# A depthwise 5x5 convolution on TensorE: 24 tiles of up to 128 pixels a plane for 25 squares of 121, and the stores issued by ACT

## What is computed

```python
def reference(x, L0_conv_kernel):           # x (128, 55, 55, 96), kernel (96, 5, 5)
    k = jnp.transpose(kernel, (1, 2, 0))[:, :, None, :]
    y = lax.conv_general_dilated(x, k, window_strides=(1, 1), padding='SAME',
        dimension_numbers=('NHWC', 'HWIO', 'NHWC'), feature_group_count=96)
    return x + y
```

## Time and profile before

| | us |
|---|---|
| median of 3 runs | 821.78 (820.1 to 821.82) |
| the profiled execution | 820.36 |
| its span, first to last instruction | 818.6 |
| PE busy in it | 811.2 (99%), 7217 products |
| POOL, ACT, DVE busy | 620.6, 617.4, 538.9 |
| mean granted TensorE clock | 0.999 |

### The profile page before, as it was taken

How to read it: one execution, slowest core, us unless ns; L and a number is a source line. 1 busy time by engine, 2 the same in 40 slices (tenths; PEclk the granted TensorE clock), 3 DMA queues, 4 the chain that set the end, 5 groups by cost and what they waited for, 6 DMA issues and landing times.

```text
span 818.6 us, 19694 instructions
## 1 busy us (share of the span) xinstructions
PE 811.2 (99%) x7217; PEld 809.2 (99%) x7217; DVE 538.9 (66%) x2224; ACT 617.4 (75%) x1157; POOL 620.6 (76%) x263
## 2 busy tenths in 40 slices
PE   8999999999999999999999999999999999999997
PEld 7999999999999999999999999999999999999997
DVE  6666666666666666666666666666666666666664
ACT  6777777777777777777777777777777777777774
POOL 2978878778696786977778878778696786977772
PEclk9999999999999999999999999999999999999999
DMA  9999999999999999999999999999999999999965
GB/s 370 418 414 393 388 387 386 392 385 396 395 389 393 375 402 388 387 391 383 395 391 391 389 386 386 395 381 395 395 387 394 380 399 381 390 390 391 389 246 232
DMA packets 32497, 313.40 MB, mean 383 GB/s; under 512 B 3600, under 2 KB 6800, under 8 KB 8080
## 3 DMA queue, kind: packets, MB, share of 16 engines
q1 hardware_dynamic: 31968, 311.67, 97.4%
q10 hardware_dynamic: 432, 0.46, 0.2%
HBM read 161.13 MB, written 150.99 MB: 381 GB/s over the span
## 4 chain that ended last, share of the span: by engine, by line
PE 98%; DMA 1%; DVE 0%; ACT 0%; ACTq 0%; issue 0%; DVEq 0%
PE sums L428 98%; DMA places_in<-places 1%; DVE x_low L254 0%; DVE weights L249 0%; DVE rest L235 0%; DVE taps_split L233 0%; DVE taps_split L237 0%; ACT y_out L323 0%; ACTq L219 0%; DVEq L163 0%; DVE y_out L357 0%; DVEq L228 0%
## 5 line engine op out<-in xcount | busy, mean ns | idle before, releaser
L428 PE MATMUL sums<-weights,x_high 121*128 121x226 f32 (+3 forms) x4800 | 804.1, 274 | 0.0
L428 PEld LDWEIGHTS sums<-weights,x_high 121*128 121x128 f32 x4800 | 729.0, 192 | 0.0
L428 PE MATMUL sums<-weights,x_low 121*128 121x226 f32 (+3 forms) x2400 | 659.1, 275 | 1.5 <-DVE x_low L254 1.5
L254 POOL TENSOR_TENSOR x_low<-x_in,x_high 121x1920 fp32r<-121x1920 f32 x95 | 411.9, 4336 | 175.3 <-ACT x_high L315 175.3
L323 ACT ACTIVATE y_out<-sums 128x264 f32<-128x264 f32 (+2 forms) x960 | 360.4, 398 | 189.8 <-PE sums L428 176.0
L428 PEld LDWEIGHTS sums<-weights,x_low 121*128 121x128 f32 x2400 | 460.8, 192 | 1.9 <-issue 1.9
L363 DVE TENSOR_TENSOR y_out<-sums,y_out 128x96 f32<-128x96 f32 (+3 forms) x1056 | 263.0, 249 | 123.3 <-ACT y_out L323 102.3
L315 ACT ACTIVATE x_high<-x_in 121x1920 fp32r<-121x1920 f32 (+1 forms) x195 | 295.2, 1514 | 5.3 <-DMA x_in<-x 5.2
L254 DVE TENSOR_TENSOR x_low<-x_in,x_high 121x1280 fp32r<-121x1280 f32 (+1 forms) x100 | 170.1, 1704 | 71.1 <-ACT x_high L315 71.1
L357 DVE TENSOR_TENSOR y_out<-sums,y_out 128x44 f32<-128x44 f32 (+2 forms) x768 | 152.0, 198 | 76.6 <-ACT y_out L323 76.3
L249 POOL TENSOR_TENSOR weights<-taps_split,places_in 121x450 fp32r<-121x450 f32 x95 | 133.7, 1407 | 7.2 <-DVE taps_split L237 7.2
(11 more groups left out here) (9 smaller groups left out, 1.9 us busy)
## 6 DMA issues: line engine op xcount, KB each, us to landing
x_in<-x SPq DMA_DIRECT2D x95, 1600.0 KB, 11.6
y<-y_out SPq DMA_DIRECT2D x95, 1536.0 KB, 7.5
taps_in<-taps SPq DMA_DIRECT2D x22, 150.0 KB, 11.8
x_in<-x SPq DMA_DIRECT2D x5, 320.0 KB, 5.3
y<-y_out SPq DMA_DIRECT2D x3, 302.5 KB, 2.5
y<-y_out SPq DMA_DIRECT2D x1, 357.5 KB, 3.7
taps_in<-taps ACTq DMA_DIRECT2D x2, 150.0 KB, 4.9
y<-y_out SPq DMA_DIRECT2D x1, 271.0 KB, 2.6
```

Source lines behind the costliest of these rows:

```text
L254: engine.tensor_tensor(x_low[slot][0:SQUARE, cols], x_in[c % X_SLOTS][0:SQUARE, cols], x_high[slot][0:SQUARE, cols].bitcast(F32), ALU.subt ...
L428: product = pe.matmul(sums, v[slot][0:SQUARE, at:at + IMAGES], window, start=n == 0 and v is x_low, stop=n == len(squares) - 1 and part == ...
```

## The change

A plane is cut into three bands of 16 rows by seven strips of 8 columns, 128 pixels each (the last strip has 7 columns), and a foot, rows 48 to 54, in three tiles of 7 x 18 = 126 pixels. One pixel column is left at the foot's right end, 7 pixels of column 54: the corner. The corner doesn't go through PE: for a group of channels at once DVE (for the first four channels POOL) multiplies its pixels with the taps and adds up, in twelve steps (a memset, five times a product and an addition, the pixels themselves), and the result is added to y_out as the last operation of every channel. 24 tiles make 72 products a channel, in 12 sums, ten copied by ACT and two by DVE. y_out is now in the plane's own order.

Windows of the blocks are 20 x 12, those of the foot 9 x 25 (written by POOL in two more operations, 25 columns in a pitch of 26). The taps' split moves from POOL to DVE, one of its three operations in each of three channels out of four. DVE's corner steps stand behind the sixth, ninth and twelfth sum of a channel: three a channel in the first four channels, one or two up to channel 11, then one in each channel up to 83, none from 84 on. The stores of all channels but the last move from SP to ACT, behind the first copy of the next channel. At the start one load brings the first taps, the centre and the block mask; the foot's mask and the corner's pixels and taps (1.08 MB) follow on ACT's queue; POOL does the twelve corner steps of the first group before its first windows and makes the last two x_low pieces of channel 0. 14 products of zeros for 17.

```diff
-SIDE = 11
-GRID = HEIGHT // SIDE
+BLOCK_H, BLOCK_W = 16, 8
+BANDS = 3
+STRIPS = 7
+FOOT = BLOCK_H * BANDS
+FOOT_H, FOOT_W = HEIGHT - FOOT, 18
+FOOT_TILES = 3
...
+GROUPS = ((0, 4), (4, 12)) + tuple((c, c + 12) for c in range(12, CHANNELS, 12))
+CORNER_STEPS = 2 + 2 * TAPS
...
+SUMS = ((0, (0, 1, 2)), (0, (3, 4)), (0, (5, 6)),
+        (1, (0, 1)), (1, (2, 3)), (1, (4, 5)), (1, (6,)),
+        (2, (0, 1)), (2, (2, 3)), (2, (4, 5)), (2, (6,)),
+        (BANDS, (0, 1, 2)))
...
-FIRST_PIECES = tuple((j, j + 1) for j in range(GRID))
-LATER_PIECES = ((0, 2), (2, GRID))
+FIRST_PIECES = ((0, 3), (3, 7), (7, 14), (14, 21), (21, 24))
+LATER_PIECES = ((0, 11), (11, 24))
...
+        def place_foot(engine, c):
...
+            for part in (HIGH, LOW):
...
+                engine.tensor_tensor(window, turned, mask, ALU.mult).then_inc(foot_ready[c % SLOTS], 1)
...
+        def sum_corner(engine, group, step):
...
+            if adds:
+                to = sums[:, :, row:end_row, :]
+                engine.tensor_tensor(to, part, to, ALU.add).then_inc(corner_step[group > 0], 1)
+            else:
...
+                engine.tensor_tensor(part, pixels[:, :, row + shift:end_row + shift].unsqueeze(3).broadcast_to(shape),
+                                     rows.unsqueeze(2).broadcast_to(shape), ALU.mult).then_inc(corner_step[group > 0], 1)
...
         @block.sync
...
-                store_y(c)
...
         @block.scalar
...
+            def store_y(c):
+
+                act.wait_ge(tile_copied, copied(c, LAST_SUM))
+                act.wait_ge(y_step, stepped(c, LAST_SUM))
+                act.dma_start(out[c, :, :], y_out[c % Y_SLOTS][:, :]).then_inc(y_stored[c % Y_SLOTS], 16)
...
                             copy_sums(c, i)
+                            if i == 0 and c > 0:
+
+                                store_y(c - 1)
...
         @block.vector
...
+                    part = corner_sum[group % GROUP_SLOTS][:, c - GROUPS[group][0], :, :]
+                    seam = y[:, HEIGHT - CORNER_ROWS:HEIGHT, WIDTH - CORNER_OUT:WIDTH]
+                    dve.tensor_tensor(seam, part, seam, ALU.add).then_inc(y_step, 1)
...
+                if c // BATCH + 1 < BATCHES and c % BATCH < SPLIT_STEPS:
+                    split_taps(dve, c // BATCH + 1, c % BATCH)
+                for i in range(len(SUMS)):
                     finish_sums(c, i)
+                    if i in (5, 8, 11) and todo:
+                        sum_corner(dve, group + 1, todo.pop(0))
```

More of the change, by code:

```diff
@@ new lines, with rows_of, cols_of, pitch_of @@
+Y_COLS = 3072
+def rows_of(i):
+    band = SUMS[i][0]
+    return max(0, band * BLOCK_H - HALO), min(HEIGHT, (band + 1) * BLOCK_H + HALO)
+def cols_of(i):
+    band, strips = SUMS[i]
+    width = FOOT_W if band == BANDS else BLOCK_W
+    return max(0, width * strips[0] - HALO), min(WIDTH, width * (strips[-1] + 1) + HALO)
+def pitch_of(i):
+    first, end = cols_of(i)
+    return end - first + (end - first) % 2
+def tiles_of(i):
+    band, strips = SUMS[i]
+    return [band * STRIPS + strip for strip in strips]
@@ L93, with copied_by_act, row_seam, col_seam @@
+def copied_by_act(i):
+    return i not in (6, 10)
+def row_seam(i):
+    return SUMS[i][0] > 0
+def col_seam(i):
+    return SUMS[i][1][0] > 0
+LAST_SUM = len(SUMS) - 1
+COPIES = [sum(copied_by_act(n) for n in range(i + 1)) for i in range(len(SUMS))]
+STEPS = [sum((not copied_by_act(n)) + row_seam(n) + col_seam(n) + (n == LAST_SUM) for n in range(i + 1))
+         for i in range(len(SUMS))]
 COPIES_ALL, STEPS_ALL = COPIES[-1], STEPS[-1]
@@ L152, in bank_of, with group_of, build @@
 def bank_of(c, i):
-    return (c * len(TILES) + i) % BANKS
-LAST_TILE = len(TILES) - 1
+    return (c * len(SUMS) + i) % BANKS
+def group_of(c):
+    return next(g for g, (first, end) in enumerate(GROUPS) if first <= c < end)
 LAST = CHANNELS - 1
-LAST_STORES = tuple((Y_AT[j], Y_AT[j + 1] if j < GRID - 1 else Y_COLS) for j in range(GRID))
-def build(nc, x, taps, places, out):
+LAST_STORES = ((6, 0, WIDTH * (2 * BLOCK_H - HALO)),
+               (10, WIDTH * (2 * BLOCK_H - HALO), WIDTH * (FOOT - HALO)),
+               (11, WIDTH * (FOOT - HALO), Y_COLS))
+def build(nc, x, taps, start, foot, corner, out):
     with ExitStack() as ctx:
@@ L173, in build @@
         y_out = [sbuf(f"y_out{i}", [P, Y_COLS], F32) for i in range(Y_SLOTS)]
[L174 to L177, removed]
+        start_in = sbuf("start_in", [P, 2 * BATCH_COLS + BLOCK_COLS], F32)
@@ L428, in tile @@
-                        product = pe.matmul(sums, v[slot][0:SQUARE, at:at + IMAGES], window,
+                        if foot_tile:
+                            window = foot_weights[slot][0:pixels, part, :, left:right]
+                        else:
+                            window = block_weights[slot][:, part, :].rearrange("p (r c) -> p r c", c=WINDOW_W)[
+                                :, above:above + end - first, left:right]
+                        product = pe.matmul(sums, v[slot][0:pixels, at:at + IMAGES], window,
@@ L443, in _ @@
                     pe.wait_ge(low_ready[slot], lows(c, piece))
[L444 to L446 removed]
+                    for i in range(len(SUMS)):
+                        if first <= tiles_of(i)[0] < end:
+                            sum_tiles(c, i)
 def lay_out_input(x):
[L450 to L451 removed]
```

436 lines of the change are left out of this document (246 added, 190 removed).

## The result

The changed kernel takes **923.29 us** (median of 4 runs, 922.75 to 923.73), the kernel before in the same comparison 821.06. The ratio is 1.1246 with a 95% interval of 1.1226 to 1.1265: 12.5% slower. The prediction was 941, with a range of 838 to 965.

The account below looks back on a forecast made before the run. PE's loads of x bound the kernel before; in the changed one a circle over ACT, POOL and DVE was expected. 9.6 + 14 + 697 + 126 + 88 + 4.6 + 1.8 = 941 us, range 838 to 965.

Parts of the forecast that it names:

- channel 0: First channel: POOL waits for the corner data, so its x_low comes after PE wants it; 14 us.
- channels 1 to 84: 70 channels with a two-operand corner step at 9.95 us, 14 with or behind a memset step at 9.0.
- The circle: Corner step waits out POOL's x_low, delaying ACT's store, x_high and the next x_low; 9.95 us a channel, chance 0.68.
- Memset channels and those behind them: 7 channels whose corner step is a memset and the 7 behind them: between 8.04 and 9.95, taken at 9.0.
- A PE clock that stays at full in spite of such gaps: Sign for the forecast: PE's clock stays full although PE waits 1.9 us once a channel.
- 24 tiles, 8.04 a channel: PE: 72 products a channel at 111.7 ns each, 8.04 us for 8.38; over 96 channels 32 us less.
- Two signs: ACT idle some 2 us before the copy behind the store; PE waiting 1.9 us a channel for a DVE seam.
- The DMA, counted at nothing: 8.04 us a channel asks for 398 GB/s; the queues were expected to give it, so nothing was counted.
- The foot's windows, 0.60 each: POOL's two new window operations: 0.60 us each, between bounds of 0.52 and 1.43.
- third rival: Foot's windows cost 1.43 us each or more, POOL and DVE share 10.3 us a channel; about 970 us, chance 0.04.
- The second rival: DVE blocked but no circle; POOL and DVE's shared SBUF time paces, 8.67 a channel, 846 us; 0.14 including mixtures.
- The first rival: Corner steps get in beside POOL or cost DVE nothing it can't catch up; 794 us, chance 0.14.

Follow-up runs that it names:

- e2: The changed kernel with DVE's corner steps moved ahead of all seams, stores still by ACT: 820.44 us, ratio 0.999 to the kernel before.
- e3: The changed kernel with the steps of DVE's corner groups replaced by memsets in the same places, from channel 4 on: 797.45 us.
- e6: The kernel before, stores by ACT, plus one DVE instruction of 252 columns a channel, both operands in SBUF, result unused: 1021.56 us.
- e8: As e6, stores by ACT, but the added instruction's first operand is in PSUM: 820.50 us.
- e1: The changed kernel with its stores issued by SP again, nothing else: 853.99 us, ratio 1.040 to the kernel before.
- e7: As e6, both operands in SBUF, but the stores stay with SP as in the kernel before: 951.49 us.
- e5: The changed kernel with corner steps ahead of the seams, a first group of 12 channels and a new start, stores by ACT: 803.72 us.
- e4: The kernel before, changed only in that ACT issues the stores behind the next channel's first copy: 821.08 us.

## Why the prediction was right, point by point

The mechanism is the one that was put down, and e2, e3, e6 and e8 show it: take away the place, the kind of instruction or the second SBUF operand, and the loss goes. The terms of the sum against what was measured in the profiled execution:

| term | predicted, us | measured, us |
|---|---|---|
| first product | 9.6 | 8.5 |
| channel 0 | 14 | 16.4 |
| channels 1 to 84 | 823 | 803.9 |
| the last 11 | 88 | 89.2 |
| tail and around the span | 6.4 | 5.5 |
| sum (the profiled execution) | 941 | 923.4 |

- **The circle, 9.95: 9.68.** The mis-sized terms are ACT's. The issue took 0.34, not 0.45. For the four copies 1.48 stood, the length of the rows end to end; but an instruction's row on ACT begins before the one ahead has ended (the four copies' row runs to 509.91, the x_high behind them starts at 509.76), so from start to start they took 1.11. x_high was 1.62 for 1.59, POOL's x_low 3.76 as computed, the corner step's end 0.25 behind it for 0.28, DVE's tail 2.38 for 2.29. The 70 channels that were taken at 9.95, by 0.27 less, make 19 us; the sum was too high by 18, so the other terms cancel nearly. The circle's lower bound, 914, held; of its two bounds, 9.6 and 10.2 for 70 channels are 916 and 958, not 914 and 962.
- **Memset channels and those behind them** were taken at 9.0 each: 8.46 and 9.03.
- **Channel 0, 14: 16.4.** POOL's start was as described, and PE waited 4.4 us once for POOL's x_low. What was not foreseen is that the clock fell there.
- **"A PE clock that stays at full in spite of such gaps"** failed at the start. The granted clock fell to half (1.2 GHz) three times in the first 130 us of the span, for 3.4 to 6.8 us; in three stretches of 4 us that end near the falls (12 to 16, 54 to 58, 122 to 126) PE had been busy for only 2.5, 2.5 and 2.4. That alone doesn't tell a fall: from 502.24 to 506.24 it was 2.50 too, and the clock stayed at full. What decides is not shown. Behind the third fall it stayed at full up to the last product, though PE was busy for 87% of the stretch from 100 to 700 us only; mean 0.992. In e6, with a longer wait each turn (PE stood 1.69 us at 512.78 there, 1.50 at 506.24 here), it fell, in parts of the run, every 20 us for 3.4, mean 0.957. There a channel of 11.95 us is followed by one of 8.7 or 8.8, together two turns of 10.33: PE's slower stretch was covered by the circle, which runs over ACT, POOL and DVE.
- **24 tiles, 8.04 a channel:** 8.05 to 8.08 where nothing holds PE up. 111.7 ns held for 240 columns too (median 112 from product to product in e3).
- **Two signs came at another size.** ACT stood idle for 2.8 and 3.4 us ahead of the copy behind the store (the turns at 499.01 and 508.65), not for some 2, and PE waited for a seam of DVE for 1.3 in the mean (98.0 us in 75 waits), not for 1.9.
- **The DMA, counted at nothing:** right, e3 moved 398 GB/s.
- **The foot's windows, 0.60 each:** 0.79 in the mean, 0.65 alone, so the third rival was far off. POOL has the room.
- **The second rival, 846 at 8.67 a channel,** came close to e1 (853.99 at 8.7), but not for its reason. It counted what DVE and POOL share as the bound; in e1 POOL still stood idle for 187 us waiting for x_high, and e7 shows that what remains without ACT's store is a circle over PE's banks, with a length of its own. That it is this circle is read from the chains of e1 and e7; no run takes it apart. The prediction had not named it, and the expectation for e7 failed on that.
- **The first rival, 794,** is what the change would have given without the exclusion: 797.45 in e3.

What stays open: the 16.4 us of channel 0 in the changed kernel were not taken apart into POOL's lateness and the clock's, and whether the last 6 us of e5 can be had by another order of DVE's three instructions wasn't tried.

## What to carry to other kernels

Before an instruction is put behind another on DVE, look for its operands: with both in SBUF it should not come up while a long instruction of POOL runs (4.00 us for 0.42 in e6); with one operand in PSUM (e8), or as a memset (e3), it was not held off at the same place. Such a stall is dear only where it closes a circle, so follow the late engine's result until it comes back: here once over the store on ACT, once over PE's banks, and the longer one sets the time. A sum of busy times, or even of the times that DVE and POOL exclude each other, finds neither; and the remedy was not to remove work or to move the store back, but to move the step some places forward in its own engine's order.

## What the runs showed of the hardware

- The exclusion goes both ways and holds for short instructions: in e2 and in e3 POOL's foot windows (0.65 alone) took 1.46 in the mean, and DVE's 27-element addition, 0.19 alone, 0.50 in e2.
- Rows of successive instructions on ACT overlap by some 0.15 us in these traces (509.91 against 509.76), so a chain is to be added from start to start.
- One core moved 398 GB/s for 600 us with loads and stores on two queues, and 95 stores on ACT's queue instead of SP's changed nothing (e4, ratio 1.0002).
